# Two recurrent blocks moved into the first expert layer's slots, with single PSUM banks there

## The reference

```python
# layer 0: conditioning, then 8 experts, the best 2 of them by a router
z = dW(fside, cond, x)                       # polynomial of degree 2 in each factor
logits = z @ Wg + bg                         # 128 -> 8, top 2 of the softmax at temperature 5
h = gelu(z @ W1[e] + b1[e])                  # 128 -> 256
x1 = x + sum_k gate_k * (h @ W2[e_k] + b2[e_k])
# layer 1: a recurrence over the 128 time steps, then shared and routed experts
h_t = tanh(x1_t @ Wx + b + h_{t-1} @ Wh)     # 32 sequences side by side
logits = layernorm(h) @ gate_w.T             # top 2 of 8
y = swiglu(h, sWg, sWu, sWd) + sum_k gate_k * swiglu(h, Wg[e_k], Wu[e_k], Wd[e_k])
out = x1 + y
```

## Time and profile before

| | us |
|---|---|
| median of 3 runs | 458.12 |
| lowest, highest | 456.72, 459.83 |
| profiled execution, its own time | 460.27 |
| its span, first to last instruction | 458.5 |
| TensorE busy in the span | 404.3 |
| VectorE, GpSimd, ScalarE busy | 337.9, 282.4, 206.4 |
| mean granted TensorE clock, share of full speed | 0.909 |

### The profile page before, as it was taken

The page is one execution under the profiler, slowest core; times in us unless marked ns, Lnnn a source line. Parts: engine busy times, 40 slices in busy tenths (PEclk is TensorE's granted clock), DMA queues, the critical chain, the costliest instruction groups (busy, mean ns, idle before and its releaser), DMA issues.

```text
span 458.5 us, 10143 instructions
## 1 busy us (share of the span) xinstructions
PE 404.3 (88%) x2428; PEld 328.4 (72%) x2428; DVE 337.9 (74%) x1299; ACT 206.4 (45%) x660; POOL 282.4 (62%) x289
## 2 busy tenths in 40 slices
PE   3699889677999999999999999998886999999950
PEld 3376555565899999966878888875675888888840
DVE  4687878388788888883767776888679777667782
ACT  1111304131777777744454554453433455555520
POOL 0536767677777777773146666665445677776670
PEclk9977766557999999999899999998989999999995
DMA  5996111115454444642101111112412353333757
GB/s 146 273 319 213 52 46 54 48 54 126 131 134 109 110 110 108 196 141 87 68 24 37 43 41 36 47 36 76 103 47 70 83 147 96 100 97 84 277 163 211
DMA packets 48150, 49.79 MB, mean 109 GB/s; under 512 B 8627, under 2 KB 37246, under 8 KB 47966
## 3 DMA queue, kind: packets, MB, share of 16 engines
q1 hardware_dynamic: 38680, 30.46, 24.9%
q0 software_dynamic: 8640, 17.84, 11.7%
q10 hardware_dynamic: 774, 0.84, 0.6%
HBM read 27.99 MB, written 21.12 MB: 107 GB/s over the span
## 4 chain that ended last, share of the span: by engine, by line
PE 70%; DVE 16%; DMA 6%; issue 5%; POOL 1%; SPq 1%; ACT 1%; DVEq 0%; POOLq 0%; ACTq 0%
PE banks L1258 58%; PE banks L1262 9%; DMA parts<-results 4%; PE banks L1347 3%; POOL results L541 1%; DMA base<-in_x 1%; DVE stream L802 1%; DVE stream L798 1%; DVE state_lo L1131 1%; DVE stream L796 1%; DVE y_row L1040 1%; DMA results<-y_row,y_dest 0%; DVE stream L793 0%; DVE act_row L1138 0%; DVE rt_d L851 0%
## 5 line engine op out<-in xcount | busy, mean ns | idle before, releaser
L541 POOL DMA_INDIRECT results<-y_row,y_dest x142 | 139.8, 984 | 61.9 <-issue 31.7
L508 POOL DMA_INDIRECT regions<-first_w,pos x64 | 62.1, 971 | 46.7 <-ACT hT L641 29.9
L508 POOL DMA_INDIRECT regions<-parts,pos x64 | 64.2, 1003 | 32.2 <-issue 32.2
L641 ACT ACTIVATE hT<-banks,pcol 128x32 f32<-128x32 f32 x128 | 36.9, 288 | 54.1 <-PE banks L1258 52.6
L623 ACT COPY act_col<-banks 128x256 f32<-128x256 f32 x146 | 54.1, 370 | 10.8 <-PE banks L1262 10.1
L700 ACT ACTIVATE silu_row<-banks 128x256 f32<-128x256 f32 x75 | 28.8, 384 | 63.2 <-PE banks L1258 63.2
L1262 PE MATMUL banks<-const_sb,act_row 128*128 128x128 f32 x292 | 56.6, 276 | 0.0
L1258 PEld LDWEIGHTS banks<-hT,wh 128*128 128x128 f32 x256 | 40.0, 191 | 23.0 <-ACT hT L641 19.4
L1262 PEld LDWEIGHTS banks<-const_sb,act_row 128*128 128x128 f32 x292 | 41.6, 143 | 19.0 <-issue 1.6
L1138 DVE TENSOR_TENSOR act_row<-silu_row,banks 128x256 f32<-128x256 f32 x75 | 31.5, 421 | 29.3 <-ACT silu_row L700 25.9
L1258 PE MATMUL banks<-hT,wh 128*128 128x32 f32 x256 | 50.4, 279 | 0.0
(11 more groups left out here) (191 smaller groups left out, 831.7 us busy)
## 6 DMA issues: line engine op xcount, KB each, us to landing
parts<-results SPq DMA_DIRECT2D x16, 512.0 KB, 5.6
hT<-regions SPq DMA_DIRECT2D x71, 65.0 KB, 1.8
wgu<-regions SPq DMA_DIRECT2D x71, 65.0 KB, 1.9
results<-y_row,y_dest POOLq DMA_INDIRECT x142
base<-in_x SPq DMA_DIRECT2D x12, 128.0 KB, 3.2
out<-base SPq DMA_DIRECT2D x20, 64.0 KB
regions<-const_sb SPq DMA_DIRECT2D x18, 65.0 KB
first_w<-in_L_ffn_W SPq DMA_DIRECT2D x1, 1024.0 KB, 8.3
```

What stands on the lines that cost most here:

```text
L508: pool.indirect_dma_start(regions[layer], bass.IndirectOffsetOnAxis(ap=poss[layer][q][:, t, k:k + 1], axis=0), hrows[layer][:, q, t, k, :] ...
L541: pool.indirect_dma_start(results[layer], bass.IndirectOffsetOnAxis(ap=y_dest[:, s:s + 1], axis=0), y_row[:, s, :], None).then_inc(results ...
L641: nc.scalar.activation(hT[:, hcols(n, step_col(s), B)], rnn_ps[:, p, step_col(s):step_col(s) + B], ACT.Tanh, bias=pcol[:, ROW_CB:ROW_CB + ...
```

## The change

- The first two recurrent blocks (32 steps) are done inside `slots0`, from slot 46 on: one step per slot, two in every fourth (`steps_in_slot`), on TensorE between `hidden_slot` and `turn_act`, the second behind `slot_down`. Their x1 sums stand between VectorE's results (`X1_AT`), their loads between SyncE's row loads (`LOAD_AT`), `turn_back(0)` at slot 44.
- The recurrence needs banks 4, 5 and 6, so in layer 0 `turned`, `act_turned` and the result have one bank each (2, 3 and 7), and their waits are for the slot before instead of the one before that. `up` keeps two.
- `stream_body` runs for blocks 2 to 7 and works on the block two before (`LAG` = 2); blocks 6 and 7 get their shared expert in `slots1`: 8 shared slots for 4, and one round of routing over both blocks (`LATE`, `LAST_ROUND`), whose pieces stand two slots later than before.
- `CUT` 1 for 2: the first table has 16 slots for 32, the second 55 for 39.
- `split_wgu` (the low parts of the weights) goes from VectorE to GpSimd, three splits behind its last result of layer 0 and five behind the first `inv_std`. Only body 7 keeps the extra matmuls that do no work.
- GpSimd sends all of block 5 and then the 16 scatters of blocks 6 and 7 among the results of slots 8 to 23 (before: 8 ahead of and 8 among slots 8 to 15). `inv_std` of the last round stands before the fourth send of block 5.
- `make_table(2)` stands behind block 5's positions, at the end of body 7; before, it stood in the middle of the body.
- In layer 1 `slot_down` is 3 slots behind for 4, and sums of finished blocks are done as halves, one a slot from slot 60 (`add_half`).

```diff
-CUT = 2
-ALL_SLOTS, FULL_SLOTS = TOPK * TOK // P + E - 1, (32, 40)
+CUT = 1
+ALL_SLOTS, FULL_SLOTS = TOPK * TOK // P + E - 1, (16, 40)
-SHARED_SLOTS = NT
+SHARED_SLOTS = len(LATE) * NT
-AHEAD, ACT_LAG, DOWN_LAG = 3, (3, 2), (5, 4)
+AHEAD, ACT_LAG, DOWN_LAG = 3, (3, 2), (5, 3)
-POST_AT = {"logits": 3, "one": 4, "two": 5, "gates": 8, "rows": 9, "ranks": 11, "blocks": 14, "slots": 16}
+POST_AT = {"logits": 5, "one": 6, "two": 7, "gates": 10, "rows": 11, "ranks": 13, "blocks": 16, "slots": 18}
+LOAD_AT, X1_AT = {54: 0, 60: 1, 64: 2}, {43: 0, 52: 1, 63: 2}
+TURN_FIRST_AT, FIRST_STEP_AT = 44, 46
+def steps_in_slot(j):
+    return 0 if j < FIRST_STEP_AT else 1 + ((j - FIRST_STEP_AT) % 4 == 2) if j < ALL_SLOTS else 1
...
-        up_ps, result_ps = banks[:, 0:2, :], banks[:, 2:4, :]
+        def result_of(layer, q):
+            return banks[:, 2 + q % 2, 0:D] if layer else bank_b[:, 0:D]
+        def turned_of(layer, r):
+            return banks[:, 4 + r % 2, 0:P] if layer else banks[:, 2, 0:P]
+        def act_turned_of(layer, q):
+            return banks[:, 6 + q % 2, 0:HID] if layer else banks[:, 3, 0:HID]
...
             def slot_down(layer, j, w, at):
                 pe.wait_ge(act_copied[layer], j + 1)
-                if j >= 2:
-                    pe.wait_ge(y_ready[layer], j - 1)
+                if j >= 1 + layer:
+                    pe.wait_ge(y_ready[layer], j - layer)
...
# TensorE, slots0
+                    if j == TURN_FIRST_AT:
+                        pe.wait_ge(rnn_w_in, 32)
                         turn_back(0)
                         hidden_slot(j, experts[j])
+                    if until > done:
+                        early_step(done)
                     if 0 <= j - act_lag < count:
                         turn_act(0, j - act_lag)
                     if j >= lag:
                         slot_down(0, j - lag, w2, experts.pop(j - lag) * HID)
+                    if until > done + 1:
+                        early_step(done + 1)
...
# VectorE, slots0
                     if j >= lag:
                         gate_result(0, j - lag, experts[k - lag])
+                    if j + 2 in X1_AT:
+                        add_one(X1_AT[j + 2])
+                    if j in X1_AT:
+                        sum_x1(X1_AT[j])
...
# GpSimd
+            for i in range(NT * TOPK):
+                if i == LAST_STD_BEHIND:
+                    inv_std(LAST_ROUND)
+                scatter1(m + i)
...
# VectorE, stream_body(i), n = i - LAG
+                if n:
+                    positions(1, n - 1, (n - 1) % 3)
+                variance1(n)
+                if n:
+                    add_shared(n - 1)
+                if i + 1 < NB:
+                    add_one(i + 1)
+                    sum_x1(i + 1)
+                multiply(n, 0)
+                logits1(n)
+                choose(1, n)
+                multiply(n, 1)
+                gates(1, n, n % 3)
+                if n == SPLIT - 1:
+                    positions(1, n, n % 3)
+                    find_blocks(2)
+                    make_table(2)
```

More of the change, by code:

```diff
@@ L169, in tiles_of @@
 def tiles_of(layer, n):
-    return NT if layer else len(GROUPS[n]) * NT
+    return len(ROUNDS[layer][n]) * NT
 def tiles_on(layer, q, n):
-    return sum(tiles_of(layer, m) for m in range(n) if m % (2 + layer) == q)
+    return sum(NT if layer else tiles_of(0, m) for m in range(n) if m % (2 + layer) == q)
 class Chain:
@@ L360, in counted_after @@
         def counted_after(layer, n):
[L361 removed]
+            return layer and {SPLIT - 1: 1, LAST_ROUND: 2}.get(n)
         def table_values(eng, d, at, count, most):
@@ L747, in _ @@
             load_tables(ACT.Silu)
-            act.wait_ge(y_ready[0], HELD_ROWS)
-            for i in range(NB):
-                if i == 1:
-                    act.wait_ge(y_ready[0], LAYER_SLOTS[0])
+            for i in range(LAG, NB):
                 stream_body(i, i % 2)
@@ L1034, in gate_result @@
                 row, y = rows[layer][:, r % ROWS_RING, :], y_row[:, s, :]
-                gate, result = row[:, D:D + 1], result_ps[:, q % 2, 0:D]
+                gate, result = row[:, D:D + 1], result_of(layer, q)
                 if layer == 0:
@@ L1400, in slots0 @@
                         turn_rows(0, j + AHEAD)
-                    if j == FIRST_TURN_AT:
-                        pe.wait_ge(state_ready[0], count)
+                    if j == TURN_FIRST_AT:
+                        pe.wait_ge(rnn_w_in, 32)
                         turn_back(0)
+                    if j == TURN_FIRST_AT + 1:
+                        for k in range(2):
+                            rnn_input(0, 0, k)
+                    done, until = steps_until(j), steps_until(j + 1)
                     if j < count:
@@ L1440, in slots1 @@
                     if q == 1:
-                        logits1(last, range(NT))
+                        late_logits()
                     if 0 <= q - act_lag < count:
@@ new lines, in stream_body @@
+                    if n and s == RANKS_AT:
+                        ranks1(n - 1)
+                    for c in range(NC):
+                        for part in range(2):
+                            if s in PAIR_AT[c][part]:
+                                pair(n, c, part, PAIR_AT[c][part].index(s))
+                    if s in LOGIT1_AT:
+                        k = LOGIT1_AT.index(s)
+                        logits1(n, (2 * k, 2 * k + 1))
+                    for c in range(NC):
+                        for k in range(2):
+                            if s == DOWN_AT[c][k]:
+                                down1(n, c, (2 * k, 2 * k + 1))
```

426 lines of the change are left out of this document (225 added, 201 removed).

## The result

| | before | after |
|---|---|---|
| median of 4 runs each, us | 458.98 | 514.22 |
| lowest, highest | 456.72, 460.54 | 508.60, 516.32 |
| profiled execution, its own time | 460.27 | 512.17 |
| its span | 458.5 | 510.3 |
| mean granted TensorE clock | 0.909 | 0.879 |

The kernel after takes 1.1155 times as long (95% interval 1.1039 to 1.1271). That ratio leaves out two of the four runs after, 516.27 and 516.32, which fell in a slower state over 1.5% above the fastest; the other two have a median of 510.4. Later runs are set against this 510.4. The prediction of 488.0 had the direction; its range ended at 505.0, 9 us short of the median of all four. The span grew by 51.8 us where I had 29.9.

A forecast was written before the change was run, and what follows sets the result against it. TensorE was taken as the bound almost everywhere; +18.9 us to the recurrence's end, +14.0 at the second layer's start and -3.0 for the rest gave +29.9, forecast as 488.0 us from the median of 458.12, range 475 to 505.

The forecast's parts named there:

- Step g: The rest, from the second layer's first routed slot to the end: -3.0 us in sum.
- d: Two blocks leave the recurrence, so body 2 starts sooner after the last first-layer `slot_down`: -27.7 us.
- e: The six recurrent bodies: body 2 waits for block 3's load, plus smaller costs: +3.4 us, ends 0 and 5.
- Step f: Start of the second layer's slots: late variance, `inv_std` and five sends delay the first routed slot: +14.0 us.
- a: Tables before the first-layer slots: first table smaller, second larger: +0.5 us.
- Step b: First-layer slots: one result bank makes a hand-off loop of 1.70 us per slot against 1.197: +35.2 us.
- Step c: The 32 early recurrent steps in the first-layer slots, partly hidden, plus stalls: +7.5 us, ends 2 and 11.
- Rival A: First-layer slots: the hand-off hides, TensorE stays the bound and the single bank costs 0: 453.6 us; chance 0.10.
- rival C: First-layer slots: TensorE idles 29% of a slot and its clock falls: +31 us, 519; chance 0.06.
- Rival B: Second layer starts on time, the variance out before GpSimd's fourth send: 479.0 us; chance 0.20.
- D: First-layer slots: tanh between gelus reloads the table, two loads in each of 26 slots: 67 us, 555; chance 0.02.

## Why the prediction missed

The direction and most steps held. The high end of the range stood for a span 46.5 us longer; it became 51.8. Step g took it out, with +6.1 where both ends had -3.0; d and e lay 1.7 and f 1.0 beyond their upper ends, and a, b and c 6.5 inside theirs. The forecast itself missed by g (9.1 us) and by the wake in b (6.6) above all.

*Step g, "the rest", failed twice.* The term was -3.0 and had no upper bound. First, I had looked at GpSimd's queue for the end of the kernel and priced it there (+1.4), not for what the scatters in it feed. With a result and a scatter in turn, 2 x 1.27 us for a slot of 1.475, the last scatter starts at 434.67, and the second table's rows come behind it: +7.2 us at the hole. Second, the saving of 3 us did not come. The choosing parts of the last router were to fall in f's wait and leave shorter holes among the first routed slots; the first 15 intervals took 33.9 us before and take 34.1 after. Behind the last routed slot the time is 1.2 us shorter where I had nothing in sum.

*Step b failed in one term.* The four parts were 0.86, 0.41, 0.28 and 0.15; measured 0.87, 0.40, 0.28 and 0.25. I took the wake from another pair of instructions, and named 0.25 as the end of the range. A tenth of a microsecond 70 times is 7 us: +41.8 instead of +35.2. Rival A, that the hand-off hides, is refuted: its threshold was 1.27 and the kernel before with one bank runs at 1.79. What "TensorE: Matmul & The Clock Gate" in the Trainium skill reports of one kernel (a second PSUM buffer without gain) does not carry over to four short passes and a three-instruction hand-off; the second bank is worth 43.9 us here. The Trainium skill, "Perfetto Trace Analysis", section "Matmuls", advises to rotate independent matmul groups through different banks, and here the trace agrees: 1.21 us with two banks, 1.79 with one.

*Step c was 2 us short.* Its parts stood where I put them: 3.89 us of VectorE at slot 41 and 1.38 of TensorE at slot 44. The lower clock behind the stands wasn't counted. Slots of after less slots of before with one bank, 135.8 - 125.7, give c as 10.1 us against 7.5, below its upper end.

*Steps d and e were 3 us short, all of it in body 2.* From the last `slot_down` it took 20.5 us where my terms give 17.5, at a granted clock of 0.69; the other bodies lasted in sum as forecast (69.4 us, 69.1). I had weighed the lower clock for the slots (rival C) and not for the recurrence. GpSimd's splits, for which I had counted nothing, do slow VectorE. While the five run (7.05 us from 260.14), its two sums take 1.64 us each, 0.68 and 0.69 in body 3:

```profile
260.31 1.64 DVE L1157 TENSOR_TENSOR parts<-base,parts 128x512 f32<-128x512 f32 x1 [1.27 <-DMA parts<-results]
261.98 1.64 DVE L1162 TENSOR_TENSOR base<-parts 128x512 f32<-128x512 f32 x1
```

But body 2 is as long without them (19.46 us for 19.51, above), so the nothing was right there.

*Step f was right in mechanism*: `rstd` 12.9 us behind block 7's rows and 14.0 behind the last tanh (about 13 predicted), then `inv_std` and five sends; the first routed slot at 26.7 instead of 24.7, because `inv_std` over eight tiles takes 1.67 us where I had taken the 1.04 of four, and turning and rounding the first rows takes 2.17 instead of 1.35, in a stage with a granted clock of 0.76; the other 0.6 is spread over the chain. Rival B (second layer on time) is refuted.

*Rivals C and D.* C did not come: in the slots at 116 to 180 the granted clock was 1.00. By the profile TensorE idled 15% of that time, though, where C counted on 29%. The clock fell at the borders instead, 0.69 and 0.76 in the rows of the first section, and behind the stand at slot 41. D is refuted: after has three table loads in all, at 2.9, 91.6 and 247.5 us, the last of them for Silu behind the last gelu, though tanh and gelu alternate in 26 slots. The Trainium skill, "ScalarE: Activation LUTs", section "Table sets: the hidden batching unit", lists a set for gelu beside those that it names for tanh; had each needed its own, there would be 52 loads in these slots, and the trace has none.

## What to carry to other kernels

A buffer that is written, taken up by another engine and given back makes a loop; add up its parts, wakes included (0.25 us here, from VectorE to TensorE), and compare with the period that you want before you give away the second buffer. If it must be single, give it back at the last instruction that reads it, not at the one that finishes the work: that was worth 20 us here. And when a queue grows, ask of each item in it who waits for it, not only when the queue ends.

## What was unexpected in the hardware

- *A VectorE sum and GpSimd's splits took turns.* A sum of 0.69 us that started 0.19 us ahead of two splits of 2.48 us together took 3.21, about the sum of both (3.17), and the splits took no longer than alone. The Trainium skill, "SBUF — State Buffer", section "Terms", calls the pair of ports that the two share a lock that is held for the whole instruction. That the times add up agrees; that the one that started first waited does not fit it so well, as far as GpSimd's times can be trusted.
- *Where the granted clock fell to its lower level of 1.2 GHz, TensorE had stood before, but not every stand brought it.* After's stand of 4.04 us at slot 41 was followed by 0.50 from 189 to 195, while idle time in every slot from 116 to 180 left it at 1.00. The lower level can last through full work: body 2 of the kernel with earlier loads was at 0.50 from 247 to 263 with TensorE busy 15.6 of 16 us. In the kernel with later splits it was 0.65 on average from 328 to 342 with TensorE busy throughout; I found no trigger for that.
- *The measured chips differ by more than the change.* Three took 551 to 556 us for the kernel before, two 457. Each was seen on one occasion only, so it is not shown that the chip is the cause. On the three that take longer, instructions have their usual lengths, but engines stand with their input there, at nearly the same slots each time, as ScalarE for 1.96 us here:

```profile
151.75 0.37 ACT L689 COPY act_col<-banks 128x256 f32<-128x256 f32 x1 [1.96 <-remote]
```

  What they wait for the trace does not say. It hides a loop of 1.79 us but for 1% of the time (562.15 for 555.72), so a change must be judged beside the kernel before on the same chip, and by its intervals.
